# The MLP's gated product on VectorE, read from PSUM, in place of a ScalarE copy and a GpSimd product

## The chip, the core and the metric

The kernel runs on one core of a Trainium2 chip, as one program. The core has five engines that run their own instruction streams and wait for each other by semaphores: TensorE (PE, with its weight loads as PEld), VectorE (DVE), ScalarE (ACT), GpSimd (POOL) and SyncE (SP, which issues DMAs). The metric is the time of one execution on the device in microseconds.

## The reference

A decoder layer for 16 sequences of 256 tokens with 256 features: a gated delta rule with its MLP, a cross attention over 120 context rows, and a mixture of eight experts, each followed by a layer norm. The part that the change touches is the MLP of the first block:

```python
h = residual + mixer_out
hn = _rmsnorm(h, norm2_w)
ffn = jax.nn.silu(hn @ wg) * (hn @ wu) @ wd
return h + ffn
```

`wg` and `wu` are 256 x 691, `wd` is 691 x 256, all in float32. The mixer before it is a scan over the tokens of each sequence (`S = a*S; pred = S k; S = S + k (b (v - pred))`), which has to go token by token.

## The kernel before

The order of the work is written out by hand: each engine has its own function in a block, and one engine's instructions run in the order in which its function issues them. No scheduler moves anything. The inner dimension of the MLP, 691, is cut in IC = 6 pieces of 128 rows (the last has 51), and `width(i)` is a piece's height.

The scan runs in two halves of 128 tokens. The first half is in `front_and_scan`, to about 580 us. `scan_and_post` runs the second half and, beside it, everything that follows the mixer for the first half's tokens; then the same for the second half's tokens, without a scan beside it; the expert part (`dispatch`, `experts`, from about 1500 us on) comes last.

`scan_and_post` works on 16 pairs of sequence halves, eight before and eight after, in a pipeline of six stages, "a b f c d e": a is the mixer's output and the norm (`residual`, `squares`, `normed`, tile `hn`), b is the MLP's gate and up products (`gate_up`) with the gating, f its down product (`down`, `mlp_out`, tile `x1`), c and d are the attention (`queries`, `score`, `maximum`, `exponential`, then `probabilities`, `values`, `second_norm`, tile `x2`), and e is the routing (`logits`, `choose`, `positions`). A pair enters a stage in each step. b is in steps 1 to 8 (first half's tokens, under the scan) and 12 to 19 (second half's). Steps 5 to 7 and 16 to 18 are loops, the others are written out.

The scan beside it is cut in 16 chunks of 8 tokens. PLAN gives the steps 0 to 10 one chunk or two: 1, 1, 1, 2, 2, 2, 2, 2, 1, 1, 1. VectorE does one token at a time in `scan_step`, called a turn here: products with the state (L137), a sum (L149), an outer product (L158), an update of the state (L168), each twice, and `next_values` (L120) or `next_keys` (L113) now and then. Each turn starts with an L137. VectorE's `step` calls `scan(0)` to `scan(15)` with the other stages' work in between; with one chunk, only each second call does anything. So the last turns of a step are `scan(14)` and `scan(15)` with two chunks, and `scan(14)` alone with one. GpSimd reads the state out after each four turns (`read_out`, L210, then L216 and L218), at VectorE's pace.

The gating of piece i: TensorE makes gate and up of the piece in the two halves of one PSUM bank, `gu(i)`, four banks in turn, so pieces 4 and 5 need the banks of 0 and 1 again (L1383 waits for that). ScalarE's `gate_out` makes silu of the gate half (L1260) and copies the up half to tile `prod` (L1261). GpSimd's `gated` multiplies the two in place (L1003), all six in one go at the end of its step, between its read-outs. `down` (L1396) of the next step reads `prod`. In the second half's tokens VectorE also scales the attention's probabilities (`normalise`, L1100): for row block 1 this is the first thing in the step after the one that made them.

The lines that the prediction uses: L1122 is VectorE's logits, L1126, L1131 and L1136 are the choice that follows, L1144 its positions, which need TensorE's counts (L1448); L1403 is TensorE's queries, which wait for ScalarE's `x1T` (L1268) and for the previous pair's logits (L1479); L1369 is TensorE's transposes of `x2` and `hn`; L1299 is ScalarE's `normed`, which needs GpSimd's `rstd` (L984); L1286 is ScalarE's `second_norm`.

## Time and profile before

| | |
|---|---|
| median of 3 runs | 2067.56 us (2066.26 to 2071.94) |
| the profiled execution | 2071.13 us, span 2069.5 us |
| busy over the span | PE 69%, DVE 64%, POOL 48%, ACT 36% |
| mean granted TensorE clock | 0.835 |

The part with the MLP in it runs from about 587 to 1440 us. In it the page's tenths for VectorE read 9 in nearly all slices to 1140 us and 3 to 1 behind, and those of TensorE read 5 to 7 to 1140 and 9 behind. The chain of work that ended last, as the page prints it, is in the expert part (TensorE 24% of the span) and says nothing of the stretch before it.

The timeline gives for an instruction its start, its length and, in brackets, how long its engine had been idle before it and what ended that. Lengths overlap: an engine starts its next instruction before the last one has written its end, so what an instruction costs its engine is the distance between two starts.

### The profile page before, as it was taken

The numbers are of one execution on the slowest core, as the hardware profiler recorded it, in microseconds if no ns is written. First come the engines' busy times: TensorE is split into PE (matmuls) and PEld (weight loads), VectorE is DVE, ScalarE is ACT, GpSimd is POOL, SyncE is SP. The second block draws the span as 40 slices with busy tenths as digits, with TensorE's granted clock in tenths as the row PEclk, the third lists the DMA queues.
The fourth block names the chain that finished last, engine by engine and source line by source line (L and its number), as shares of the span: only waits on it lengthen the run. The fifth ranks groups of instructions, "written<-read, shape, count | busy, mean of one in ns | idle before, by whom it ended". The sixth has DMA issues, their size and how long they took to land. (4 is left out here: it accounts for less than half of the span.)

```text
span 2069.5 us, 28474 instructions
## 1 busy us (share of the span) xinstructions
PE 1419.1 (69%) x6660; PEld 983.3 (48%) x6661; DVE 1328.2 (64%) x3231; ACT 755.0 (36%) x2412; POOL 999.8 (48%) x1213
## 2 busy tenths in 40 slices
PE   6424448400025666676775899998669999999997
PEld 5313336300024455455554677776535555555554
DVE  4699999999989999999878124334323232223232
ACT  5511114401102555564676377776401111111111
POOL 3267777776668877777567523432111111111111
PEclk9756779855558878787886999999779999999998
DMA  4501114600031000010000212142240320320300
GB/s 125 196 11 31 42 32 132 239 0 0 0 128 35 20 25 18 23 34 24 25 25 16 97 35 60 40 128 75 69 128 21 120 90 20 131 84 21 101 18 6
DMA packets 97685, 125.41 MB, mean 61 GB/s; under 512 B 10001, under 2 KB 74952, under 8 KB 95560
## 3 DMA queue, kind: packets, MB, share of 16 engines
q1 hardware_dynamic: 60040, 97.22, 14.8%
q10 hardware_dynamic: 33136, 18.58, 3.1%
q0 software_dynamic: 4432, 8.73, 1.2%
q8 instruction: 30, 0.49, 0.1%
q14 instruction: 47, 0.39, 0.1%
HBM read 89.68 MB, written 35.74 MB: 61 GB/s over the span
## 5 line engine op out<-in xcount | busy, mean ns | idle before, releaser
L210 POOL TENSOR_TENSOR wt<-wt 128x1024 f32<-128x1024 f32 x128 | 301.1, 2352 | 152.0 <-DVE wt L168 152.0
L216 POOL TENSOR_TENSOR wt<-wt 128x512 f32<-128x512 f32 (+2 forms) x384 | 322.6, 840 | 30.1
L1846 PE MATMUL e_ph<-wt,e_g 128*128 x624 | 274.4, 593 | 0.0
L168 DVE SCALAR_TENSOR_TENSOR wt<-wt,scan 128x256 f32<-128x256 f32 x512 | 241.5, 472 | 0.1
L158 DVE TENSOR_TENSOR scan<-scan,wt 128x256 f32<-128x256 f32 x512 | 220.3, 430 | 19.7 <-DVE wt L168 14.1
L149 DVE TENSOR_REDUCE scan<-wt 128x16 f32<-128x272 f32 x512 | 222.2, 434 | 0.1
L1244 ACT ACTIVATE wt<-p_pX,p_mx 128x120 f32<-128x120 f32 x512 | 176.0, 379 | 101.9 <-DVE p_mx L1089 101.6
L137 DVE TENSOR_TENSOR wt<-wt,scan 128x256 f32<-128x256 f32 x512 | 208.6, 407 | 4.7 <-PEq L233 4.7
L1375 PE MATMUL p_pm<-p_w_mix,p_oT 128*128 128x256 f32 x128 | 43.9, 502 | 240.7 <-DMA p_oT<-o 210.0
L1739 POOL TENSOR_TENSOR e_ve<-e_mv,eps 128x1 f32<-128x1 f32 x39 | 7.4, 189 | 375.4 <-DVE e_mv L1790 375.4
L1846 PEld LDWEIGHTS e_ph<-wt,e_g 128*128 128x128 f32 x624 | 115.6, 190 | 130.8 <-issue 130.8
L1884 PE MATMUL e_ph<-wt,e_xT 128*128 x312 | 150.0, 605 | 3.7 <-DVE e_xT L1765 3.6
L1375 PEld LDWEIGHTS p_pm<-p_w_mix,p_oT 128*128 128x128 f32 x128 | 30.6, 251 | 250.9 <-issue 244.4
L1811 ACT ACTIVATE e_g<-e_pT 128x512 f32<-128x512 f32 x39 | 23.3, 597 | 342.4 <-PE e_pT L1861 342.4
L692 PE MATMUL f_pT<-ident,f_xn 128*128 128x128 f32 x64 | 15.2, 381 | 170.9 <-ACT f_xn L564 121.7
L1089 DVE TENSOR_REDUCE p_mx<-p_pX 128x8 f32<-128x960 f32 x64 | 72.9, 1149 | 92.5 <-PE p_pX L1418 92.3
L1386 PE MATMUL p_pX<-p_hT,p_wg 128*128 128x256 f32 (+1 forms) x384 | 111.7, 418 | 15.3 <-ACT wt L1244 15.3
L1780 DVE TENSOR_TENSOR e_h<-e_ph,wt 128x512 f32<-128x512 f32 x78 | 54.0, 692 | 102.3 <-PE e_ph L1884 102.3
L1396 PE MATMUL p_py<-p_wd,p_prod 128*128 128x256 f32 (+1 forms) x384 | 108.9, 431 | 12.3 <-DVE p_place L1144 8.0
L1244 ACT ACTIVATION_READ_ACCUMULATOR wt<-p_pX,p_mx 128x1 f32 x512 | 115.7, 226 | 0.0
L1386 PE MATMUL p_pX<-p_hT,p_wu 128*128 128x256 f32 (+1 forms) x384 | 104.1, 396 | 0.0
L1396 PEld LDWEIGHTS p_py<-p_wd,p_prod 128*128 128x128 f32 (+1 forms) x384 | 75.0, 209 | 44.4 <-issue 35.1
(212 smaller groups left out, 2987.6 us busy)
## 6 DMA issues: line engine op xcount, KB each, us to landing
wt<-in_L_ffn_W SPq DMA_DIRECT2D x24, 1024.0 KB, 5.3
qkv<-f_st ACTq DMA_DIRECT2D x48, 256.0 KB, 2.3
p_kE<-kE SPq DMA_DIRECT2D x16, 480.0 KB, 3.7
p_vP<-vP SPq DMA_DIRECT2D x16, 480.0 KB, 4.5
e_xt<-routed ACTq DMA_DIRECT2D x39, 130.0 KB, 2.1
f_xt<-in_x SPq DMA_DIRECT2D x16, 256.0 KB, 3.0
f_raw_k<-qkv SPq DMA_DIRECT2D x4, 1024.0 KB, 5.2
f_raw_q<-qkv SPq DMA_DIRECT2D x4, 1024.0 KB, 7.9
```

Source lines behind the costliest of these rows:

```text
L137: nc.vector.tensor_tensor(s["sk"][:, h, u % V, :, 0:HD], s["S"][:, h, (u - 1) % R], s["kn"][:, h, u % KN:u % KN + 1].to_broadcast([P, HD, ...
L149: nc.vector.tensor_reduce(s["w"][:, h], s["sk"][:, h, u % V], AX, ALU.add).then_inc(s["w_done"], 1)
L158: nc.vector.tensor_tensor(s["outer"][:], s["w"][:, h].rearrange("p (v o) -> p v o", o=1).to_broadcast([P, HD, HD]), s["k"][:, h, bass.ds(c ...
L168: nc.vector.scalar_tensor_tensor(s["S"][:, h, u], s["S"][:, h, (u - 1) % R], s["gate"][:, jb, h, 1, bass.ds(c * R + u, 1)], s["outer"][:], ...
L210: nc.gpsimd.tensor_tensor(x, s["S"][:, h, z * Q:(z + 1) * Q], s["q"][:, h, now].rearrange("p t (o d) -> p t o d", o=1).to_broadcast([P, Q, ...
L216: nc.gpsimd.tensor_tensor(x[:, :, :, 0:half], x[:, :, :, 0:half], x[:, :, :, half:2 * half], ALU.add).then_inc(s["o_fold"][h], 1)
L1244: ins = nc.scalar.activation(pr[:, x // 2, head], scores(x)[:, y // 4, y % 4], ACT.Exp, bias=mx[:, x // 2, head:head + 1], accum_out=sm[:, ...
L1375: ins = nc.tensor.matmul(dst[:, q], rows[:, g, q * P:(q + 1) * P], wt[:, g], start=(g == 0), stop=(g == G - 1))
L1386: ins = nc.tensor.matmul(gu(i)[0:c, which], wt[:, g, i * P:i * P + c], hT[:, g], start=(g == 0), stop=(g == G - 1))
L1396: ins = nc.tensor.matmul(py[:, q], prod[0:c, i, q * P:(q + 1) * P], wd[0:c, i], start=(i == 0), stop=(i == IC - 1))
L1846: ins = nc.tensor.matmul(ph2[:], g1[:, c // (C1 // 2), c % (C1 // 2)], wt[:, bass.ds(at_b + (W2_AT + c * F2), F2)], start=(c == 0), stop=( ...
L1884: ins = nc.tensor.matmul(ph1[:, q], xT[:, g], wt[:, bass.ds(at + (W1_AT + g * F1 + q * HALF), HALF)], start=(g == 0), stop=(g == G - 1))
```

## The change

VectorE gets a function `gated(b, i)`, which multiplies the silu in tile `gate` with the up half in PSUM into `prod`; it is called for pieces 0 and 1 before `scan(14)`, for 2 and 3 before `scan(15)`, and for 4 and 5 at the end of the step. It waits for its gate, and its first call for `down` of the pair before. ScalarE's copy and GpSimd's `gated` are gone. Three waits change: ScalarE's first gate of a step waits for the last step's products (the tile `gate` is free then), TensorE's `gate_up(4)` waits for products 0 and 1 in place of gates 0 and 1, and TensorE's step starts behind all six products in place of all gates.

```diff
--- before.py
+++ after.py
@@ -996,12 +996,6 @@
                 pool.wait_ge(rs_done, n * 3 + 2)
                 nc.gpsimd.tensor_tensor(shift[:, which], k["empty"][:, 0:2], scaled_mean[:, which], ALU.subtract).then_inc(rs_done, 1)
 
-            def gated(b):
-                for i in range(IC):
-                    c = width(i)
-                    pool.wait_ge(gate_done, (b * IC + (i + 1)) * 2)
-                    nc.gpsimd.tensor_tensor(prod[0:c, i], prod[0:c, i], gate[0:c, i], ALU.mult).then_inc(prod_done, 1)
-
             def doubled(a):
                 pool.wait_ge(h_done, a + 1)
                 if since(a, 1):
@@ -1035,8 +1029,6 @@
                     inverse_rms(a)
                     doubled(a)
                 outputs(4 if full else 1, len(parts) - 2)
-                if "b" in on:
-                    gated(b)
                 outputs(len(parts) - 2, len(parts))
 
             steps(pool, step)
@@ -1138,6 +1130,13 @@
 
                 dve.wait_ge(choice, chose(e, CHOSEN))
                 nc.vector.tensor_tensor(total[:, 1], total[:, 0], chosen[:, 0], ALU.add).then_inc(choice, 1)
+
+            def gated(b, i):
+                c = width(i)
+                dve.wait_ge(gate_done, b * IC + (i + 1))
+                if i == 0 and since(b, 1):
+                    dve.wait_ge(down_done, b * 2)
+                nc.vector.tensor_tensor(prod[0:c, i], gate[0:c, i], gu(i)[0:c, 1], ALU.mult).then_inc(prod_done, 1)
 
             def positions(e):
                 dve.wait_ge(count_done, e + 1)
@@ -1212,8 +1211,17 @@
                 scan(13)
                 if "c" in on:
                     inverse_sums(c, 1)
+                if "b" in on:
+                    gated(b, 0)
+                    gated(b, 1)
                 scan(14)
+                if "b" in on:
+                    gated(b, 2)
+                    gated(b, 3)
                 scan(15)
+                if "b" in on:
+                    gated(b, 4)
+                    gated(b, 5)
 
             steps(dve, step)
 
@@ -1256,9 +1264,8 @@
                 c = width(i)
                 act.wait_ge(gu_done, b * IC + (i + 1))
                 if i == 0 and since(b, 1):
-                    act.wait_ge(down_done, b * 2)
+                    act.wait_ge(prod_done, b * IC)
                 nc.scalar.activation(gate[0:c, i], gu(i)[0:c, 0], ACT.Silu).then_inc(gate_done, 1)
-                nc.scalar.activation(prod[0:c, i], gu(i)[0:c, 1], ACT.Copy).then_inc(gate_done, 1)
 
             def copied(n, done, out, used, dst, src):
 
@@ -1380,7 +1387,7 @@
                 if i == 0:
                     pe.wait_ge(hT_done, (b + 1) * G)
                 if i == 4:
-                    pe.wait_ge(gate_done, (b * IC + 2) * 2)
+                    pe.wait_ge(prod_done, b * IC + 2)
                 for which, wt in enumerate((wg, wu)):
                     for g in range(G):
                         ins = nc.tensor.matmul(gu(i)[0:c, which], wt[:, g, i * P:i * P + c], hT[:, g], start=(g == 0), stop=(g == G - 1))
@@ -1468,7 +1475,7 @@
                 if "c" in on or "d" in on or "b" in on:
 
                     if since(b, 1):
-                        pe.wait_ge(gate_done, b * (2 * IC))
+                        pe.wait_ge(prod_done, b * IC)
                     if since(c, 1):
                         pe.wait_ge(exp_done, c * HALVES)
                     if since(d, 1):
```

At three places on VectorE. First the end of step 1 (one chunk; `wt` and `scan` hold the scan's state), before:

```order
L168 SCALAR_TENSOR_TENSOR wt<-wt,scan 128x256 [waits s_outer_done]
L113 TENSOR_TENSOR scan<-wt 128x128 [waits s_sk_done]
L149 TENSOR_REDUCE scan<-wt 128x16 [waits s_sk_done]
L137 TENSOR_TENSOR wt<-wt,scan 128x16x16 [waits s_kn_done,s_S_done]
L158 TENSOR_TENSOR scan<-scan,wt 128x256 [waits s_w_done]
```

and after:

```order
L168 SCALAR_TENSOR_TENSOR wt<-wt,scan 128x256 [waits s_outer_done]
L113 TENSOR_TENSOR scan<-wt 128x128 [waits s_sk_done]
L149 TENSOR_REDUCE scan<-wt 128x16 [waits s_sk_done]
L1139 TENSOR_TENSOR p_prod<-p_gate,p_pX 128x256 [waits p_gate_done] x3
L1139 TENSOR_TENSOR p_prod<-p_gate,p_pX 51x256 [waits p_gate_done]
L137 TENSOR_TENSOR wt<-wt,scan 128x16x16 [waits s_kn_done,s_S_done]
```

Four products stand now between the end of the last turn (L149) and the first instruction of the next step's first turn (L137), each behind a wait for its gate. The second place is before turn 14 in the looped steps 5 to 7, before:

```order
L149 TENSOR_REDUCE scan<-wt 128x16 [waits s_sk_done]
L1096 RECIPROCAL p_rc<-p_sm 128x16 [waits p_norm_done,p_exp_done]
L134 REGISTER_ALU
L137 TENSOR_TENSOR wt<-wt,scan 128x16x16 [waits s_S_done]
L158 ISA [waits s_w_done]
L158 TENSOR_TENSOR scan<-scan,wt 128x256
```

and after (L1088 is L1096 of before):

```order
L149 TENSOR_REDUCE scan<-wt 128x16 [waits s_sk_done]
L1088 RECIPROCAL p_rc<-p_sm 128x16 [waits p_norm_done,p_exp_done]
L1136 ISA
L1139 TENSOR_TENSOR p_prod<-p_gate,p_pX 128x256 [waits p_down_done,p_gate_done]
L1136 REGISTER_ALU
L1139 TENSOR_TENSOR p_prod<-p_gate,p_pX 128x256 [waits p_gate_done]
L134 REGISTER_ALU
L137 TENSOR_TENSOR wt<-wt,scan 128x16x16 [waits s_S_done]
L158 ISA [waits s_w_done]
```

Products 0 and 1 stand between the sums' reciprocal and the turn. The third place is the end of the looped steps 16 to 18, without a scan, before:

```order
L1115 REGISTER_ALU
L1117 TENSOR_SCALAR p_x<-p_x 128x2 [waits p_row_out]
L1096 RECIPROCAL p_rc<-p_sm 128x16 [waits p_norm_done,p_exp_done]
L864 REGISTER_ALU
L864 COMPARE_AND_BRANCH
L1100 TENSOR_TENSOR wt<-wt,p_rc 128x1920 [waits p_rec_done]
L1122 TENSOR_TENSOR p_lg<-p_pq,p_br 128x16 [waits p_choice,p_logit_done]
```

and after (L1092 is L1100 of before, L1114 is L1122):

```order
L1139 TENSOR_TENSOR p_prod<-p_gate,p_pX 128x256 [waits p_gate_done]
L1136 REGISTER_ALU
L1139 TENSOR_TENSOR p_prod<-p_gate,p_pX 128x256 [waits p_gate_done]
L1136 REGISTER_ALU
L1139 TENSOR_TENSOR p_prod<-p_gate,p_pX 51x256 [waits p_gate_done]
L864 REGISTER_ALU
L864 COMPARE_AND_BRANCH
L1092 TENSOR_TENSOR wt<-wt,p_rc 128x1920 [waits p_rec_done]
L1114 TENSOR_TENSOR p_lg<-p_pq,p_br 128x16 [waits p_choice,p_logit_done]
```

The last three of six products are shown: they stand ahead of the loop's branch, and `normalise` and the logits of the next round come behind them.

## Rows read from the trace of the kernel before

**Rows 1.** Stretches: busy us (instructions) of PE, PEld, DVE, ACT, POOL; clock, DMA share.

```profile
640.00:1053.00 413.00, 279.00 (x1451) 214.02 (x1451) 392.93 (x1000) 225.70 (x811) 318.25 (x372) 0.80 0.09 25
1330.06:1367.78 37.72, 37.19 (x250) 29.86 (x249) 15.06 (x32) 28.58 (x105) 14.10 (x20) 1.00 0.21 68
```

**Rows 2.** Who VectorE waited for, 606 to 1014 us: us in total, times, longest.

```profile
DVE p_h L1064 <- PE p_pm L1375: 0.9, 1, 0.9
```

**Rows 3.** Instructions on tile prod, whole run: ns min/median/max.

```profile
L1261 ACT ACTIVATE p_prod<-p_pX x96: 364/378/430, 635.7 to 1412.5; 128x256 f32<-128x256 f32 x80, 51x256 f32<-51x256 f32 x16
L1003 POOL TENSOR_TENSOR p_prod<-p_prod,p_gate x96: 713/725/1017, 641.8 to 1412.9; 128x256 f32<-128x256 f32 x80, 51x256 f32<-51x256 f32 x16
```

**Rows 4.** Timeline of VectorE, end of step 6: start us, us, instruction [idle before].

```profile
926.23 0.41 DVE L137 TENSOR_TENSOR wt<-wt,scan 128x256 f32<-128x256 f32 x1
926.56 0.47 DVE L168 SCALAR_TENSOR_TENSOR wt<-wt,scan 128x256 f32<-128x256 f32 x1
...
927.46 0.36 DVE L137 TENSOR_TENSOR wt<-wt,scan 128x256 f32<-128x256 f32 x1
```

**Rows 5.** Timeline of ScalarE, step 6: gates 0, 4 and 5.

```profile
917.64 0.38 ACT L1260 ACTIVATE p_gate<-p_pX 128x256 f32<-128x256 f32 x1
...
924.77 0.38 ACT L1260 ACTIVATE p_gate<-p_pX 128x256 f32<-128x256 f32 x1 [1.60 <-PE p_pX L1386]
...
926.63 0.38 ACT L1260 ACTIVATE p_gate<-p_pX 51x256 f32<-51x256 f32 x1 [1.20 <-PE p_pX L1386]
```

**Rows 6.** Timeline of TensorE, step 6: queries.

```profile
870.52 3.78 PE L1403 MATMUL p_pq<-p_x1T,p_wq 128*128 128x256 f32 x8 [10.50 <-DVE p_lg L1122]
```

**Rows 7.** Timelines, ends of steps 1 and 2.

```profile
639.27 0.41 DVE L137 TENSOR_TENSOR wt<-wt,scan 128x256 f32<-128x256 f32 x1
...
643.50 0.38 ACT L1260 ACTIVATE p_gate<-p_pX 51x256 f32<-51x256 f32 x1 [1.20 <-PE p_pX L1386]
...
666.56 0.91 ACT L1299 ACTIVATE p_hn<-p_h,p_rstd 128x256 f32<-128x256 f32 x2 [2.29 <-POOL p_rstd L984]
...
667.99 2.25 DVE L113 TENSOR_TENSOR scan<-wt 128x128 f32<-128x128 f32 x1
...
670.49 0.41 DVE L137 TENSOR_TENSOR wt<-wt,scan 128x256 f32<-128x256 f32 x1
...
673.88 0.38 ACT L1260 ACTIVATE p_gate<-p_pX 51x256 f32<-51x256 f32 x1 [1.20 <-PE p_pX L1386]
```

**Rows 8.** Timeline of VectorE, step 9.

```profile
1052.94 0.17 DVE L1122 TENSOR_TENSOR p_lg<-p_pq,p_br 128x16 f32<-128x16 f32 x1 [3.26 <-PE p_pq L1454]
...
1063.42 0.17 DVE L1144 TENSOR_TENSOR p_place<-p_py,p_chosen 128x16 f32<-128x16 f32 x1 [3.12 <-PE p_py L1448]
```

**Rows 9.** Timelines of GpSimd and VectorE at the start of step 6.

```profile
864.42 2.14 POOL L1003 TENSOR_TENSOR p_prod<-p_prod,p_gate 128x256 f32<-128x256 f32 x3
866.52 2.33 POOL L210 TENSOR_TENSOR wt<-wt 128x1024 f32<-128x1024 f32 x1
866.99 2.00 DVE L120 TENSOR_TENSOR wt<-wt 128x64 f32 x1
```

**Rows 10.** VectorE's groups, 587 to 1140 us: busy us, mean ns, idle before.

```profile
L120 DVE TENSOR_TENSOR wt<-wt 128x64 f32<-128x64 f32 (+1 forms) x62 | 44.5, 718 | 0.0
L113 DVE TENSOR_TENSOR scan<-wt 128x128 f32<-128x128 f32 (+1 forms) x31 | 21.5, 694 | 0.0
```

**Rows 11.** Timelines after the scan, steps 16 and 17.

```profile
1292.08 2.16 DVE L1100 TENSOR_TENSOR wt<-wt,p_rc 128x1920 f32<-128x1920 f32 x1 [0.26 <-DVE p_rc L1096]
...
1295.87 0.65 PE L1369 MATMUL p_py<-ident,p_x 128*128 128x128 f32 x4 [0.38 <-ACT p_x L1286]
...
1300.94 0.38 ACT L1260 ACTIVATE p_gate<-p_pX 51x256 f32<-51x256 f32 x1 [1.20 <-PE p_pX L1386]
...
1302.04 0.18 DVE L1122 TENSOR_TENSOR p_lg<-p_pq,p_br 128x16 f32<-128x16 f32 x1 [7.81 <-PE p_pq L1454]
...
1303.24 1.97 PE L1403 MATMUL p_pq<-p_x1T,p_wq 128*128 128x256 f32 x8
```

## The prediction

> **What bounds the kernel now.** I read the stretches by engine first, then who VectorE waits for, then the timeline of three of the pipeline's steps. The part that the change touches has two regimes. While the second half of the scan runs (587 to 1138 us), VectorE is busy 392.93 of 413 us in the middle stretch, ScalarE 225.70 and GpSimd 318.25 [rows 1]. From 606 to 1014 us VectorE waited for another engine once, for 0.9 us [rows 2]. So until step 8 whatever VectorE gets on top is added to the end. After the scan, a step of the loop takes 37.72 us and TensorE is busy 37.19 of them [rows 1]: there only TensorE's own gaps can be won or lost. The expert part behind it is not touched.
>
> **Part by part: what goes.** ScalarE loses 96 copies of 0.378 us (it issues one per 0.27), GpSimd 96 products of 0.725 us, 4.35 us a step [rows 3]. Under the scan neither engine sets the end, so by itself this is worth nothing there, except where a GpSimd product blocks VectorE (below).
>
> **What comes.** VectorE gets 96 products, 48 of them under the scan, one input in SBUF, one in PSUM, 128x256. The row nearest to it is the scan's L137, also SBUF times PSUM into SBUF: 0.41 us long, and the next instruction starts 0.33 us after it [rows 4]. 48 x 0.33 = 15.8 us; by the full length it would be 19.7. I take 0.33, since a product has no follower on VectorE that needs its result. The Trainium skill ("VectorE: DVE Perf Modes", The TRN2 errata) gives 120 + 256 cycles at 0.96 GHz for a PSUM source, 0.39 us; with that as the spacing the 48 would be 18.8 us; the row's spacing is shorter, and the sum goes by the row.
>
> **Waits in the two-chunk steps (3 to 7).** Products 0 and 1 stand before turn 14 (927.46), 2 and 3 before turn 15, 4 and 5 behind it. Gate 0 was made at 917.64 [rows 4, 5]: no wait. TensorE's gate_up(4) now waits for product 1, so it can't start before 928.2; at 1.9 us for each gate_up (926.63 - 924.77) gates 4 and 5 follow at about 930.2 and 932.1 [rows 5]. Their products come at about 935.8 (927.46 plus two turns, 6.97, plus four products, 1.3): again no wait. Who waits behind the later gates: ScalarE's normalise, the copy x1T (now at about 938.5) and TensorE's queries. But the queries have been waiting 10.50 us for VectorE's logits [rows 6], which come after the next step's first turn, here at about 940 (935.8 + 0.6 for the products + 4.7 for the turn, less a shorter hold, below). So 5.5 us of that cover are used and about 1.5 are left. Price: 5 steps x 6 x 0.33 = 9.9 us.
>
> **Waits in the one-chunk steps.** Here products 2 to 5 stand together, directly before the next step. Step 1: the next turn began at 639.27. Gate 5 was issued at 643.50 [rows 7]; two copies less (0.53) bring it to 642.97, its end to 643.35. Product 5 starts at 643.43 and the turn at 643.76: +4.5 us, of which 2.0 are products and 2.5 a wait. Step 2: the turn began at 670.49, after L113 had been held until 670.24 by GpSimd; the first two products vanish in that hold. Gate 5 was issued at 673.88 and nothing hurries it (its gate_up runs behind hn, which waited for GpSimd's rstd): product 5 at 674.3, turn at 674.65: +4.2 us [rows 7]. Step 8: product 5 would be made at about 1052.4 and logits come 3.2 us later than 1052.94. But in step 9 VectorE waits 3.12 us for TensorE's counts, on a chain over ScalarE's normalise and x1T that these products don't lengthen [rows 8]. I count step 8 as 0 (it would be 3.2 without that cover).
>
> **The port.** VectorE's instructions with both inputs in SBUF are held while GpSimd reads: L120 took 2.00 us at 866.99, until GpSimd's L210 had ended, which the six products had pushed back to 866.52 [rows 9]. In the stretch the 62 L120 took 44.5 us where a free one takes about 0.26, and the 31 L113 21.5 where it is about 0.29 [rows 10]: 28.4 + 12.5 us of hold; the router's small instructions with two SBUF inputs (L1126, L1136) are held too. The new product has one input in SBUF, and L137, its like, is never stretched: it pays nothing. The products that go hold VectorE little themselves; what counts is the alignment. At each of five boundaries L210 now starts some 1.3 us earlier against the scan and L120 falls behind it into L216: 0.7 us less; turn 14's L120 may win 0.4. In four of the five the router's L1126 then meets the second L210: up to 2.1 more, minus 0.9 at L1131 and L1136. Sum between -10 and +2; I take -3, since gains and losses alternate. The Trainium skill ("SBUF — State Buffer", the shared port pair) says that the pair is an exclusive lock for a whole instruction, and that one SBUF input doesn't contend; the rows above agree. Read alone, that rule makes a gain of freeing the port; that is the second rival.
>
> Scan in sum: 4.5 + 4.2 + 9.9 - 3 = +15.6 us.
>
> **After the scan.** Two things in each looped step. Gain: ScalarE's copies before second_norm go, so p_x is there 0.5 us sooner and TensorE's 0.38 us gap at L1369 goes; gate 5 comes about 0.5 sooner than 1300.94. Loss: on VectorE the six products now stand in front of the next step's L1100 (2.16 us), which ran at 1292.08, beside everything, and of logits. Product 5 at 1300.9, L1100 from 1301.2 to 1303.3, logits at 1303.3 instead of 1302.04, and queries, which ran at 1303.24, wait for logits: 1303.5 [rows 11]. The half microsecond is lost again, and 0.3 more, in five boundaries: +1.4. In the first steps of this half, where no L1100 or no logits are due, about the same is won (TensorE's down waits for a faster product). Sum 0, between -3 and +4.
>
> **Against the run's own time.** The profiled run took 2071.13 us with a span of 2069.5; with 15.6 more it would be 2086.7. It is the upper end of the shown runs, 3.6 above their median; I add the sum to the median, 2067.56: 2083.2.
>
> **Rivals.** *(1) The price is paid, as above*: 2083, with its own range of 2074 to 2092. *(2) Faster: the freed port.* All these holds are GpSimd against VectorE; if at all five boundaries and in turn 14 the collisions go (1.7 at L120 and about 1.8 at the router and turn 14, 17 us in five steps), if product 4 and 5 in steps 1 and 2 don't wait (5 less) and TensorE keeps its 0.5 us in eight steps (4 less), the sum is 18.6 - 17 - 4 = -2.4: 2065. It decides where the gain per two-chunk step passes 3.3 us; against it: GpSimd's L210 and L216 remain, and follow VectorE's own pace. *(3) The cover of 1.5 us is too thin.* If x1T comes after the logits, each two-chunk step loses the excess; a chain later by 4 us (a table load, a slower TensorE clock) costs 2.5 x 5 = 12.5 us more: 2096. For it: TensorE's clock is 0.80 here [rows 1], and gate_up(4) and (5) run directly behind an idle stretch. *(4) No difference:* the scan's steps win at the port about what they pay there (about 10), and the waits in steps 1 and 2 are partly made good by later holds that get shorter (about 4): 2069.
>
> **How the numbers follow.** Rival 1 has 0.64, 2 has 0.08, 3 has 0.14, 4 has 0.14. 0.3% is 6.2 us, about what a measurement of this kernel can tell from no change. Faster by more is the far part of rival 2: 0.05. Same, the rest of it, rival 4 and the low edge of the first: 0.18. Slower: 0.77. The range leaves out rival 2, most of what is below 4's upper edge, and the far end of rival 3: 2071 to 2095.
>
> **What would show it.** In the profile of the changed kernel: products of about 0.41 us, 0.33 apart, none waiting in the looped scan steps; a wait of about 2.5 us for gates in step 1 and about 2.9 in step 2; the scan's end some 15 us later; L120 in total nearer to 40 us than to 44.5; the wait for counts in step 9 gone or near 0; looped steps after the scan of 38.0 us with a wait for logits before the queries. Wrong would be: looped steps longer than 39 us or shorter than 37.3, a VectorE wait for counts or maxima in steps 4 to 7 (rival 3), or two-chunk steps that don't grow (rivals 2 and 4).

## The result and the profile after

The changed kernel takes 2079.61 us (median of 8 runs, 2078.01 to 2083.92), the kernel before 2070.64 us beside it (8 runs, 2066.26 to 2073.53): 1.0049 times the time before, 95% interval 1.0037 to 1.0061. It is slower by 9 us or 0.5%; 2083.2 was forecast, 15.6 us more than before. The kernel before took 3.1 us more in these runs than the 2067.56 us on which the forecast stands. The profiled execution has a span of 2080.9 us, against 2069.5.

To see where the 11.4 us between the two spans arise, take the start of the first L137 of each step on VectorE (the first turn of the scan), in the kernel before and after, and the length of each step from these (us):

| step | 0 | 1 | 2 | 3 | 4 | 5 | 6 | 7 | 8 | 9 | 10 | sum |
|---|---|---|---|---|---|---|---|---|---|---|---|---|
| before | 25.62 | 26.62 | 31.22 | 62.01 | 64.27 | 68.80 | 68.86 | 68.90 | 43.11 | 48.72 | 39.85 | 547.98 |
| after | 25.60 | 30.94 | 33.39 | 61.31 | 64.38 | 71.18 | 71.19 | 68.25 | 48.79 | 42.36 | 39.95 | 557.34 |
| change | 0 | +4.3 | +2.2 | -0.7 | +0.1 | +2.4 | +2.3 | -0.7 | +5.7 | -6.4 | +0.1 | +9.4 |

Another 0.7 us were there before step 0, in a part that the change doesn't touch, and 1.3 come behind the scan. Step 1 grew as forecast and step 8 is given back in step 9, as forecast. The two-chunk steps, 3 to 7, were to grow by 2 us each: 3, 4 and 7 did not grow, 5 and 6 did, but, as will be seen, not by the products.

VectorE's groups in the stretch of the scan (587.7 to 1150 us), which answer to [rows 10]: busy us, mean ns, idle before.

```profile
L120 DVE TENSOR_TENSOR wt<-wt 128x64 f32<-128x64 f32 (+1 forms) x62 | 31.0, 500 | 0.0
L1139 DVE TENSOR_TENSOR p_prod<-p_gate,p_pX 128x256 f32<-128x256 f32 (+1 forms) x48 | 17.7, 404 | 7.8 <-ACT p_gate L1268 7.8
L113 DVE TENSOR_TENSOR scan<-wt 128x128 f32<-128x128 f32 (+1 forms) x31 | 17.6, 566 | 0.0
```

48 products of 0.40 us are there, as forecast, and L120 and L113 are 13.5 and 3.9 us shorter than in [rows 10]: 17.4 us, where the prediction had 3.

The timeline of VectorE at the end of step 5, where the next step's first turn begins with an L137 (start, length, in brackets the idle time before), and the first turn of step 7:

```profile
867.30 0.74 DVE L1139 TENSOR_TENSOR p_prod<-p_gate,p_pX 128x256 f32<-128x256 f32 x2
867.96 0.41 DVE L137 TENSOR_TENSOR wt<-wt,scan 128x256 f32<-128x256 f32 x1
...
871.22 0.73 DVE L1139 TENSOR_TENSOR p_prod<-p_gate,p_pX 128x256 f32<-128x256 f32 x2
874.55 0.42 DVE L137 TENSOR_TENSOR wt<-wt,scan 128x256 f32<-128x256 f32 x1 [2.60 <-issue]
...
876.00 0.26 DVE L120 TENSOR_TENSOR wt<-wt 128x64 f32 x1
...
945.74 0.42 DVE L137 TENSOR_TENSOR wt<-wt,scan 128x256 f32<-128x256 f32 x1 [2.74 <-issue]
```

Two products take 0.66 us from one start to the next (867.30 to 867.96), so 0.33 each, and wait for nothing. L120, 2.00 us long at this place in [rows 9], is 0.26. New are the idle stretches of 2.60 and 2.74 us in front of the first turns of steps 6 and 7, which no semaphore explains ("issue"). In the kernel before VectorE has none there. Both stand where VectorE's loop over steps 5 to 7 returns to its start. The page's part on queues shows something too, first of the kernel before and then of the one after (packets, MB):

```profile
q14 instruction: 47, 0.39, 0.1%
```

```profile
q14 instruction: 58, 0.48, 0.1%
```

11 more packets of about 8 KB of instructions were loaded. The traces have the time of each. In the kernel before, this queue loads nothing between 856.6 and 1008.6 us, while the loop over steps 5 to 7 runs its second and third round. In the changed kernel ten packets of 8 KB start between 867.9 and 985.5 us, and one of them in each idle stretch: at 872.39 us (0.49 us long) and at 943.70 us (0.38).

The ends of steps 1 and 2, answering to [rows 7]. The last product of step 1 waits 1.43 us for its gate, the last two of step 2 wait 1.28 and 1.55 us, and L113, 2.25 us long before, takes 1.57:

```profile
641.28 1.24 DVE L1139 TENSOR_TENSOR p_prod<-p_gate,p_pX 128x256 f32<-128x256 f32 x3
643.95 0.41 DVE L1139 TENSOR_TENSOR p_prod<-p_gate,p_pX 51x256 f32<-51x256 f32 x1 [1.43 <-ACT p_gate L1268]
...
671.53 1.57 DVE L113 TENSOR_TENSOR scan<-wt 128x128 f32<-128x128 f32 x1
...
675.38 0.42 DVE L1139 TENSOR_TENSOR p_prod<-p_gate,p_pX 128x256 f32<-128x256 f32 x1 [1.28 <-ACT p_gate L1268]
677.34 0.41 DVE L1139 TENSOR_TENSOR p_prod<-p_gate,p_pX 51x256 f32<-51x256 f32 x1 [1.55 <-ACT p_gate L1268]
```

After the scan a looped step takes 38.04 us, the distance of two of ScalarE's table loads, and TensorE's queries wait for the logits, as forecast:

```profile
1300.19 1.28 ACT L1268 ACT_TABLE_LOAD   x1
1338.23 1.28 ACT L1268 ACT_TABLE_LOAD   x1
```

```profile
1311.38 1.99 PE L1410 MATMUL p_pq<-p_x1T,p_wq 128*128 128x256 f32 x8 [0.82 <-DVE p_lg L1114]
```

If each instruction of VectorE is charged with the distance to the next one's start, less the idle time named in the trace, the scan's 9.36 us close like this (us, whole scan; the kernels of the last two columns come from the experiments below):

| | before | after | after, 83 increments | after, up half in SBUF |
|---|---|---|---|---|
| products | 0 | 16.2 | 16.0 | 51.5 |
| waits of products for gates | 0 | 7.8 | 10.2 | 1.7 |
| L120 and L113 | 57.5 | 41.0 | 40.4 | 39.8 |
| the router's instructions | 28.3 | 25.2 | 26.3 | 26.4 |
| waits for TensorE | 21.1 | 19.1 | 17.1 | 13.7 |
| idle, "issue" | 0 | 5.5 | 0 | 0.5 |
| turns and the rest | 441.0 | 442.4 | 441.1 | 439.5 |
| sum | 547.98 | 557.34 | 551.23 | 573.01 |

### The profile page after: what moved, and what is told of

It is laid out like the page before. It is cut to its first block and busy times, and to the rows that moved or that the text cites. A ratio compares the mean times of both kernels' runs of the same rounds, so it can differ in the third digit from the quotient of the medians.

```text
span 2080.9 us, 28387 instructions
## 1 busy us (share of the span) xinstructions
PE 1420.1 (68%) x6660; PEld 981.2 (47%) x6661; DVE 1343.1 (65%) x3327; ACT 729.4 (35%) x2316; POOL 924.1 (44%) x1117
## 5 line engine op out<-in xcount | busy, mean ns | idle before, releaser
L210 POOL TENSOR_TENSOR wt<-wt 128x1024 f32<-128x1024 f32 x128 | 301.2, 2353 | 181.6 <-DVE wt L168 181.6
L216 POOL TENSOR_TENSOR wt<-wt 128x512 f32<-128x512 f32 (+2 forms) x384 | 322.6, 840 | 30.1
L149 DVE TENSOR_REDUCE scan<-wt 128x16 f32<-128x272 f32 x512 | 221.9, 433 | 0.1
L137 DVE TENSOR_TENSOR wt<-wt,scan 128x256 f32<-128x256 f32 x512 | 208.7, 408 | 10.1 <-issue 5.3
L1393 PE MATMUL p_pX<-p_hT,p_wg 128*128 128x256 f32 (+1 forms) x384 | 116.7, 432 | 52.1 <-DVE p_prod L1139 35.0
L1393 PEld LDWEIGHTS p_pX<-p_hT,p_wg 128*128 128x128 f32 (+1 forms) x384 | 74.3, 204 | 78.8 <-DVE p_prod L1139 36.5
L1403 PE MATMUL p_py<-p_wd,p_prod 128*128 128x256 f32 (+1 forms) x384 | 102.1, 410 | 6.3 <-DVE p_place L1143 4.2
```

Of the source, the lines that this page charges most:

```text
L137: nc.vector.tensor_tensor(s["sk"][:, h, u % V, :, 0:HD], s["S"][:, h, (u - 1) % R], s["kn"][:, h, u % KN:u % KN + 1].to_broadcast([P, HD, ...
L149: nc.vector.tensor_reduce(s["w"][:, h], s["sk"][:, h, u % V], AX, ALU.add).then_inc(s["w_done"], 1)
L210: nc.gpsimd.tensor_tensor(x, s["S"][:, h, z * Q:(z + 1) * Q], s["q"][:, h, now].rearrange("p t (o d) -> p t o d", o=1).to_broadcast([P, Q, ...
L216: nc.gpsimd.tensor_tensor(x[:, :, :, 0:half], x[:, :, :, 0:half], x[:, :, :, half:2 * half], ALU.add).then_inc(s["o_fold"][h], 1)
L1393: ins = nc.tensor.matmul(gu(i)[0:c, which], wt[:, g, i * P:i * P + c], hT[:, g], start=(g == 0), stop=(g == G - 1))
L1403: ins = nc.tensor.matmul(py[:, q], prod[0:c, i, q * P:(q + 1) * P], wd[0:c, i], start=(i == 0), stop=(i == IC - 1))
```

## The experiments

Three questions: what are the two idle stretches, why do the two-chunk steps not grow by the products, and do the halves add up? The ratios are to the kernel before, which was measured beside each group of runs; intervals are at 95%. Its median was 2070.64 us beside the changed kernel, and 2069.84, 2072.05 and 2071.11 beside the groups below, so a difference of medians across groups is uncertain by 1 to 2 us, and the ratios tell more.

**The two stretches.** The changed loop has 353 instructions on VectorE, the one before 340. The theory is that the return has to load instructions again. The first run moves the loop by increments of a semaphore that nobody reads:

```diff
@@ block.vector, front_and_scan @@
         def _(dve):
+            for _ in range(110):
+                dve.sem_inc(pads, 1)
             dve.wait_ge(set_up, SETUPS)
```

> The changed kernel with 110 semaphore increments put at the very start of VectorE's program, where it has nothing to do, so that its loop over steps 5 to 7 (353 instructions now, 340 before) begins 110 instructions later. Theory (the loop's return has to load instructions again, and where the loop begins decides it): the two idle stretches of 2.60 and 2.74 us in front of L137 at 874.55 and 945.74 us, put down to issue, are gone; last turn of the scan 5.3 us earlier than in the changed kernel, time 2074 to 2075 us, 1.002 of the kernel before. Rival (the stretches come from what the instructions wait for, or from the loop's registers): they stay, time 2079 to 2080 us.

Measured: 2081.56 us, 1.0057 (1.0044 to 1.0070). Nothing was gained. The increments cost something themselves: VectorE's first work that others wait for came at 11.97 us, in the changed kernel at 8.26. Both stretches are still there, 5.8 us together, with a packet of instructions in each, and the instruction queue carries 59 packets. The place that I had chosen was no cure. The same increments in the kernel before, 60 of them:

> The kernel before, nothing of the change, with 60 semaphore increments at the start of VectorE's program. Theory of instruction loading: the loop of 340 instructions now lies where a return has to load again; two idle stretches of 2.6 to 2.7 us appear in front of the first turn of steps 6 and 7, time 2076 us (+5.3, 1.0026). Rival (the stretches belong to the change's products or gates): none appears, 2070 to 2071 us.

Measured: 2075.25 us, 1.0025 (1.0015 to 1.0036), 5.4 us more. Two stretches appear, in a kernel without anything of the change:

```profile
867.14 0.42 DVE L137 TENSOR_TENSOR wt<-wt,scan 128x256 f32<-128x256 f32 x1 [2.37 <-issue]
...
938.43 0.42 DVE L137 TENSOR_TENSOR wt<-wt,scan 128x256 f32<-128x256 f32 x1 [2.32 <-issue]
```

```profile
q14 instruction: 58, 0.48, 0.1%
```

So it is where the loop lies in VectorE's instructions that makes the stretches, not what the change computes. Here too a packet starts in each, at 865.08 and 936.38 us. The rule of the place was still open. The Trainium skill ("Runtime: NRT & Kernel Launch", Instruction fetch mechanics) says that instructions are loaded in blocks of 16 KiB, 256 instructions, that two are held, and that a taken branch to a target outside of them stalls. That a return stalls and loads again, the runs bear out: 2.3 to 2.9 us a return, and packets in the stretches (872.39 and 943.70 us above). The sizes don't fit: with pieces of 256 the first run's loop and the one of the changed kernel can't both lie on three of them while the loop before lies on two, whatever the first one's offset. The packets are of 8 KB, so I tried pieces of 128 instructions, four of them held, one of which is loaded ahead: then a loop may lie on three pieces. Counted from VectorE's first instruction the loop starts at 1250 (before, 340 long, no stretch), 1310 (60 increments, stretch), 1277 (after, 353 long, stretch) and 1387 (110 increments, stretch). The unknown offset of the first piece can be 53 to 74 for all four to come out so, and for each of these offsets 83 increments put the start at position 5 to 26 of a piece, from where 353 instructions end on the third.

```diff
@@ block.vector, front_and_scan: in three places where VectorE waits @@
+            for _ in range(40):
+                dve.sem_inc(pads, 1)
             dve.wait_ge(set_up, SETUPS)
...
+            for _ in range(28):
+                dve.sem_inc(pads, 1)
             dve.wait_ge(small_in, 16 * NSMALL)
             nc.vector.tensor_scalar(n1[:], n1[:], ...)
+            for _ in range(15):
+                dve.sem_inc(pads, 1)
```

> The changed kernel with 83 semaphore increments on VectorE, put in three places where it waits at the program's start (40, 28 and 15). With 110 the two idle stretches stayed, with 60 in the kernel before they appeared, and the instruction queue carried 58 or 59 packets instead of 47 each time. If instructions are kept in pieces of 128 (packets of 8 KB), four of them at a time with one being loaded ahead, the five starts seen so far leave only starts at which 83 more instructions put the loop of 353 on three pieces: both stretches gone, 47 or 48 packets, time 2074 to 2075 us (-5.3 against the changed kernel). Rival (any loop of 353 instructions has to load again, wherever it begins): both stay, 2079 to 2081 us.

Measured: 2076.35 us, 1.0026 (1.0016 to 1.0037), above the 2074 to 2075 us that were named: 3.3 us less than the changed kernel by the medians and 4.8 by the ratios, where 5.3 were expected. The trace shows it plainly: the scan takes 551.23 us in place of 557.34, steps 5 and 6 68.15 and 68.36 in place of 71.18 and 71.19. The same place as above, no idle time in front of the turn:

```profile
869.92 0.73 DVE L1146 TENSOR_TENSOR p_prod<-p_gate,p_pX 128x256 f32<-128x256 f32 x2
870.57 0.41 DVE L137 TENSOR_TENSOR wt<-wt,scan 128x256 f32<-128x256 f32 x1
...
871.97 0.26 DVE L120 TENSOR_TENSOR wt<-wt 128x64 f32 x1
```

```profile
q14 instruction: 49, 0.40, 0.1%
```

The stretches are the price of loading instructions again, 2.3 to 2.9 us a return. The later kernels agree with the same rule, each with its own start and length: the stretches are in those whose loop starts at 1275 and 1277, and not in those at 1250, 1357 and 1360. Pieces of 128 are a rule that fits twelve kernels, not one that was seen.

**Why the two-chunk steps don't grow.** Take the same place again. GpSimd, in the run with the 83 increments:

```profile
869.72 2.36 POOL L210 TENSOR_TENSOR wt<-wt 128x1024 f32<-128x1024 f32 x1 [3.58 <-DVE wt L168]
```

Before, GpSimd's six products pushed L210 to 866.52, onto VectorE's L120, which it held for 1.74 us [rows 9]. Now L210 starts as soon as VectorE's turn allows (2.25 us before L120, against 0.47), and beside it stand two products, 0.73 us at 869.92, which it doesn't hold. Two things could have made L120 free: that GpSimd's products are gone, or that VectorE's products stand before it. To part them, GpSimd was given six products of other data back, which nobody reads, with VectorE's left as they are:

```diff
+            def beside(b):
+                for i in range(IC):
+                    c = width(i)
+                    pool.wait_ge(gate_done, b * IC + (i + 1))
+                    if i or since(b, 1):
+                        pool.wait_ge(beside_done, b * IC + i)
+                    nc.gpsimd.tensor_tensor(spare[0:c], bo[0:c], bo[0:c], ALU.mult).then_inc(beside_done, 1)
...
+                if "b" in on:
+                    beside(b)
                 outputs(len(parts) - 2, len(parts))
```

> The changed kernel, to which GpSimd's six products of a pair are given back at their old place, made of other data (the bias row with itself, into a spare tile) that nobody waits for; VectorE's products stay as they are. Theory (GpSimd's products held the shared port, and VectorE's copies L120 and L113 lost 1.1 to 1.8 us at each boundary of steps to them): the long L120 and L113 come back, steps 3 to 8 grow by 1.5 to 2 us each, last turn of the scan 9 to 12 us later than in the changed kernel; time 2089 to 2092 us. Rival (those copies became short because VectorE reaches them later, not because GpSimd has less to do): nothing comes back, 2080 to 2082 us.

Measured: 2084.24 us, 1.0065 (1.0047 to 1.0083), between the two: the scan is 4.5 us longer than in the changed kernel, not 9 to 12. Here the idle stretches lay over the place in question in two steps, so the run was made again with the increments:

> The run with GpSimd's idle products once more, now with the 83 increments, so that the 2.6 us at the loop's returns no longer lie over the place in question. Theory, corrected: what cost VectorE time at the boundaries was not GpSimd's products but its L210, which they pushed from beside VectorE's last turn onto the copy L120 of the next step's first turn (before: L210 866.52 to 868.85, L120 866.99 to 868.99). With the idle products L210 is pushed there again at every boundary of two-chunk steps, the two returns included: L120 of 1.5 to 2.0 us in front of steps 4 to 8, last turn 7 to 9 us later than with the increments alone, time 2083 to 2086 us. Rival (it is chance how the engines meet; the 4.5 us of the earlier run are all there is): 2080 to 2081 us.

Measured: 2080.82 us, 1.0051 (1.0038 to 1.0064), 4.5 us above the run with the increments alone; the scan is 3.8 us longer (555.07), steps 3 to 7 together 4.8. That is the rival's time: my corrected theory was too large as well. L120 comes back at the boundary, but only in part:

```profile
877.60 0.97 DVE L123 TENSOR_TENSOR wt<-wt 128x64 f32 x1
```

(L123 is L120 here, and L213 is L210.) On GpSimd:

```profile
876.09 2.35 POOL L213 TENSOR_TENSOR wt<-wt 128x1024 f32<-128x1024 f32 x1
```

It held the copy for its last 0.84 us only, since VectorE came to the copy 1.51 us after GpSimd's start, and not 0.47. Of these 1.04 us, 0.66 are the two products that stand in front of it now; the rest was not taken apart. Of the hold of 1.74 us, 0.7 are there again with GpSimd's products (0.97 less the free 0.26), and 1.0 are not, though GpSimd works as before: VectorE's own products stand, for the most part, where VectorE would have been held anyway. In L120 and L113 together, 17.1 us less than before with the increments alone, 7.7 are given back with GpSimd's idle products (in the whole scan, from the same account as above: 57.5, 40.4, 48.1); in steps 3 to 7, where 12.3 us are gone, 4.2 come back.

The other half of this account is that the product itself isn't held. In the next run ScalarE's copy of the up half is kept, with its wait for `down`, and VectorE multiplies two tiles in SBUF, at the same places, again with the 83 increments:

```diff
-                dve.wait_ge(gate_done, b * IC + (i + 1))
-                if i == 0 and since(b, 1):
-                    dve.wait_ge(down_done, b * 2)
-                nc.vector.tensor_tensor(prod[0:c, i], gate[0:c, i], gu(i)[0:c, 1], ALU.mult).then_inc(prod_done, 1)
+                dve.wait_ge(copy_done, b * IC + (i + 1))
+                nc.vector.tensor_tensor(prod[0:c, i], gate[0:c, i], prod[0:c, i], ALU.mult).then_inc(prod_done, 1)
...
                 if i == 0 and since(b, 1):
                     act.wait_ge(prod_done, b * IC)
+                    act.wait_ge(down_done, b * 2)
                 nc.scalar.activation(gate[0:c, i], gu(i)[0:c, 0], ACT.Silu).then_inc(gate_done, 1)
+                nc.scalar.activation(prod[0:c, i], gu(i)[0:c, 1], ACT.Copy).then_inc(copy_done, 1)
```

> With the 83 increments: ScalarE still copies the up half into SBUF, and VectorE multiplies gate and copy there, both from SBUF, at the same places; GpSimd makes no product. Theory (VectorE's operation on two SBUF tiles is held while GpSimd runs L210, the product from PSUM beside L210 was not): products 4 and 5, which lie beside L210 (0.73 us at 871.22 beside L210 871.03 to 873.40), take up to 2 us longer, in all two-chunk steps 5 to 10 us; last turn 5 to 10 us later than with the increments alone, time 2081 to 2087 us. Rival (a source in SBUF instead of PSUM costs nothing here, each product is even some 0.05 us shorter): 2074 to 2077 us.

Measured: 2106.69 us, 1.0171 (1.0157 to 1.0185), 30 us above the run with the increments, far more than expected. VectorE and GpSimd at the same place:

```profile
885.40 3.83 DVE L1144 TENSOR_TENSOR p_prod<-p_gate,p_prod 128x256 f32<-128x256 f32 x2
```

```profile
885.21 2.35 POOL L210 TENSOR_TENSOR wt<-wt 128x1024 f32<-128x1024 f32 x1 [5.19 <-DVE wt L168]
```

3.83 us for two products where it was 0.73 beside the same L210. The 48 products under the scan take 1147 ns in the mean, 404 with the up half in PSUM, and each two-chunk step is 4.4 to 4.7 us longer. I had thought of the first product's wait for L210 alone; the second is held once more by the read-outs that follow (L216), and so are products at other places. The Trainium skill ("SBUF — State Buffer", Who interferes with whom) says that a VectorE instruction with two SBUF inputs contends with a GpSimd instruction that reads SBUF, and that this is an exclusive lock. These rows agree. Of the 30 us, 21.8 lie in the scan (573.01 us against 551.23): so much is it worth there that the product reads one side from PSUM. The other 8.5 lie behind the scan, where there are no read-outs and a product takes 465 ns in the mean: a looped step takes 38.97 us there, with ScalarE's copies back, and this part was not taken apart.

**The two halves.** The products on VectorE for the first eight pairs alone (all under the scan), and for the last eight alone; ScalarE's copy and GpSimd's product are back for the others. Each was built from one text that has both ways:

```diff
+PAIRS = lambda b: b < 8      # the other kernel: b >= 8
...
-                if "b" in on:
+                if "b" in on and on_vector(jb, b):
                     gated(b, 0)
                     gated(b, 1)
```

> VectorE makes the products of the first eight pairs, which lie beside the scan; from the ninth pair on ScalarE's copy and GpSimd's product are back. If the two halves of the change add up: the last turn of the scan about 10.1 us later than in the kernel before, as in the changed kernel (two idle stretches of 2.6 us at the loop's returns included, since the loop has the same 353 instructions at the same place), the steps after the scan 37.7 us as before; time 2079 to 2080 us, 1.0043. Rival (what was prepared late at the end of the scan is given back after it): 2073 to 2076 us.

Measured: 2080.61 us, 1.0052 (1.0038 to 1.0067). The scan takes 556.86 us, the looped steps after it 37.73. That is what was expected, but for a time 0.6 us above the range.

> VectorE makes the products of pairs nine to sixteen alone, after the scan; the first eight are made as in the kernel before. If the halves add up: scan as in the kernel before, each step of the loop after it 38.0 us instead of 37.7, the queries waiting 0.7 to 0.8 us for the logits behind VectorE's last product and normalisation; time 2071 to 2073 us (+1.3). Rival (ScalarE's and GpSimd's relief is worth more than the late logits): 2068 to 2070 us.

Measured: 2071.61 us, 1.0007 (0.9999 to 1.0016), +1.8 us by the medians, with looped steps of 38.11 us. From the last turn of the scan to the end it takes 935.34 us, before 934.49 and in the changed kernel 935.81: +0.9 and +1.3. The interval takes in no change, so that this half costs anything rests on the traces. Within their intervals the halves add up (0.52% and 0.07%, the whole change 0.49%), and the scan's is nearly all.

**The waits for gates.** Products 4 and 5 moved behind the next step's first turn (after the scan: its `normalise`), before the logits (`on_vector` and `DEFER` are true in this run):

```diff
                 scan(0)
+                if "f" in on and on_vector(jb, f) and DEFER:
+                    gated(f, 4)
+                    gated(f, 5)
                 if "e" in on:
                     logits(e)
...
                 scan(15)
-                if "b" in on:
+                if "b" in on and on_vector(jb, b) and not DEFER:
                     gated(b, 4)
                     gated(b, 5)
```

> The changed kernel with products 4 and 5 of a pair moved on VectorE behind the first turn (after the scan: the normalisation) of the next step. Theory: the waits for the last two gates, 1.43 us in step 1 and 1.28 and 1.55 us in step 2, are gone, and after the scan the normalisation fills the waits of 1.84 and 1.43 us, so that the queries no longer wait 0.7 to 0.8 us for the logits: scan 4.3 us shorter, each of five steps after it about 0.8 us shorter; time 2071 to 2073 us. Rival (TensorE's scores, which wait for the products, come late now and give it back): 2077 to 2081 us.

Measured: 2072.82 us, 1.0010 (1.0002 to 1.0019): 6.8 us less than the changed kernel by the medians and 8.1 by the ratios, near the upper end of the range that was named. No product waits for a gate under the scan; steps 1 and 2 take 28.59 and 31.33 us instead of 30.94 and 33.39. After the scan the looped steps take 37.18 us, 0.5 less than in the kernel before, and the queries wait for nothing:

```profile
1293.37 1.28 ACT L1288 ACT_TABLE_LOAD   x1
...
1330.55 1.28 ACT L1288 ACT_TABLE_LOAD   x1
```

```profile
1303.72 1.97 PE L1434 MATMUL p_pq<-p_x1T,p_wq 128*128 128x256 f32 x8
```

**A version that beats both.** The experiments say what to keep: the old way for the first two pairs (steps 1 and 2, where the products wait and nothing hides them), VectorE's products from the third pair on, products 4 and 5 moved only after the scan, and 93 increments for the loop's place.

```diff
+PAIRS = lambda b: b >= 2
+DEFER = lambda b: b >= 8
```

> ScalarE's copy and GpSimd's product for the first two pairs, VectorE's products from the third pair on, products 4 and 5 deferred after the scan as in the run beside it, and 93 semaphore increments at the program's start so that the loop does not load again (if the pieces are of 128). Theory: steps 1 and 2 as in the kernel before, steps 3 to 9 together 2.5 us shorter, after the scan 2.7 us shorter: 2064 to 2067 us, 0.998 of the kernel before. Rivals: with the two stretches at the loop's returns 2070 us; if the steps after the scan do not gain, 2067 to 2069 us.

Measured: 2066.46 us, 0.9972 (0.9961 to 0.9982), 5.6 us less than the kernel before beside it (2072.05 us). The scan takes 543.84 us, 4.1 less than before, with steps 1 and 2 as before (26.67, 31.27), and 2.7 us are won after it (931.84 us from the last turn to the end). By the account of VectorE, its 36 products take 11.7 us of the scan and L120 and L113 are 12.8 us shorter. The 4.1 us are no measure of what the scan wins, since the run with the last eight pairs alone, whose scan is the old one, takes 544.24 us for it. Steps 3 to 7 together are 0.3 us shorter than before, and 8 and 9 are 3.3 shorter (88.58 against 91.83 us); in the run with the old scan these two take 90.25 us. What is sure is the total of 5.6 us by the medians.

## Why the prediction was right, and where its sizes were off

**The direction and the mechanism held.** The scan's half sets the time (scan alone 1.0052, rest alone 1.0007), VectorE is the bound there, and each product costs the 0.33 us that were taken from L137's spacing [rows 4]: 16.2 us for 48, where 15.8 were forecast. The figure of the Trainium skill ("VectorE: DVE Perf Modes", The TRN2 errata), taken as the spacing, would have given 18.8.

**Step 1** was worked out almost to the end: +4.5 forecast, +4.3 measured. Its parts fit less well than the sum: 2.0 us of products and a wait of 2.5 were named, and it is 2.2 of products, a wait of 1.43 and 0.6 of longer holds (L120 and L113 take 3.5 us in the step, 2.9 before), which come before the gate and so take their time out of the wait.

**Step 2** was to cost 4.2 and cost 2.2. The wait came as forecast (1.28 and 1.55, in sum 2.83 for 2.9). What I missed is that its L120 and L113, as [rows 7] showed them held (2.25 us at 667.99), are shifted too: they fell from 5.8 to 3.0 us in the step. The prediction had let the first two products vanish in one such hold, and no more.

**Steps 3 to 7** were to pay 9.9 us for products less a share of 3. They paid 9.8 for products, and got 12.4 back in L120 and L113 and 1.4 in the router's instructions. The failed term is the port's: -3, with bounds of -10 and +2, worked out for these steps; it was -13.8 there, and -16.5 for the whole scan in L120 and L113 (by the distances of the account; 17.4 by their lengths), outside of the bounds. The step of it that failed is "L210 now starts some 1.3 us earlier and L120 falls behind it into L216: 0.7 us less". L120 falls behind L210, but into nothing: it is 0.26 us. I had moved GpSimd by the products that it loses and had not moved VectorE's L120 by the two products that it gains, though they stand right in front of it, and had taken from [rows 9] that a copy beside L216 is held. With both shifts the hold is gone whole in the run with the 83 increments; with GpSimd's products back, 0.7 of its 1.74 us are. (In the changed kernel itself the loop's return moves L120 of steps 6 and 7 by another 2.6 us.) The prediction's second rival saw this gain (17 us at the boundaries and turn 14), and it got 0.08; its sum of -2.4 leaves out the 5 us that it names for steps 1 and 2. Two signs for being wrong came true: two-chunk steps that don't grow, with L120 at 31.0 us where 40 was named, and a wait of VectorE for TensorE's maxima in step 4, with which rival 3 was to show:

```profile
752.75 1.16 DVE L1081 TENSOR_REDUCE p_mx<-p_pX 128x8 f32<-128x960 f32 x1 [1.05 <-PE p_pX L1425]
```

The changed kernel waits there once, and the run with the 83 increments not at all.

**What was not in the prediction at all** is the return of the loop, 5.3 us idle and 6 us by the run that removes it. It covered nearly half of the port's miss; without it the time would have been 2076.35, and the forecast 6.9 us too high. A second piece of luck is the kernel before itself: it was forecast from 2067.56 us and takes 2070.64 beside the changed kernel. The change costs 9 us where 15.6 were forecast, and the 3.1 us hide half of that. So 2083.2 is nearer to 2079.61 than its terms are to theirs.

**Step 8** cost nothing in the end: +5.7 and, in step 9, -6.4. It waited 3.5 us for its last two gates; the wait of 3.26 us for the router's product [rows 8] was gone and the one for the counts fell from 3.12 to 2.11 us. **After the scan** 0 was forecast and +1.3 came, with looped steps of 38.04 us for 38.0, and the wait for logits for the reason given.

**The cover in the two-chunk steps** was as thin as forecast, but little hung on it. In the changed kernel the queries of step 7 wait 4.59 us for the logits, where 10.50 stood in step 6 before [rows 6], and 2.7 of them are the loop's return. In the run with the 83 increments, without that return, they wait for ScalarE's x1T:

```profile
949.08 3.35 PE L1410 MATMUL p_pq<-p_x1T,p_wq 128*128 128x256 f32 x7 [4.59 <-DVE p_lg L1114]
```

```profile
943.19 3.75 PE L1417 MATMUL p_pq<-p_x1T,p_wq 128*128 128x256 f32 x8 [2.78 <-ACT p_x1T L1282]
```

So the cover of 1.5 us was used up there, which is the condition of rival 3. Its price did not follow: VectorE waits for TensorE nowhere in steps 3 to 7 of that run, and they take 0.5 to 0.7 us less than before each. What VectorE needs from TensorE next (counts, then maxima) comes late enough in its step.

## What to carry to other kernels

When work moves between engines, move both sides of every collision: the engine that loses instructions arrives sooner and the one that gains them arrives later, and a hold of 1.7 us that was there before is time in which new instructions can stand for nothing. What is moved to VectorE beside a busy GpSimd should read one input from PSUM (404 ns a product here, 1147 with both in SBUF). A change that lengthens a loop body can cost several us by where the loop lies: look for idle time put down to issue at the loop's return, and count the packets of the instruction queue, before the new instructions are blamed.

## What the runs showed of the hardware

- A return of VectorE's loop cost 2.3 to 2.9 us in six kernels and nothing in the others, and 60 increments in front of a loop that was otherwise untouched made the difference (5.4 us). The instruction queue's packets, 47 to 50 without and 58 or 59 with, tell the two apart, and in the changed kernel one of them starts inside each idle stretch (872.39 and 943.70 us). An increment of a semaphore on VectorE took some 0.1 us (with 110 of them at the program's start, VectorE's next instruction comes 11.4 us later).
- The same kernel can find TensorE at either level of its clock in one place. At step 8 the profile of the kernel before has gate_up at 1.2 GHz, and the one with the products of the last eight pairs alone at 2.4 GHz, after idle times of 3.10 and 3.09 us (in front of the transposes that come first) that don't differ, with a granted clock of 0.77 and 0.88 in the 15 us from 1040:

```profile
1045.81 1.92 PE L1386 MATMUL p_pX<-p_hT,p_wg 128*128 128x256 f32 x4
```

```profile
1042.80 1.03 PE L1417 MATMUL p_pX<-p_hT,p_wg 128*128 128x256 f32 x4
```

  The two profiles have the same instructions in the scan, yet its length is 547.98 and 544.24 us: 3.7 us, as much as several of the effects weighed here. The medians of many runs are what counts, and a step in which TensorE was waited for should not be compared between two single profiles. What decides the level there stays open.
